# The experts' opening: the second batch's first group normalized by VectorE, its second group's statistics a block later, weight low parts in three pieces

## What is computed

```python
x = x + _L0_attn_ref(_layernorm(x), ...)      # Mamba block and MLP
x = x + _L0_ffn_ref(_layernorm(x), ...)       # table weights
x = x + _L1_attn_ref(_layernorm(x), ...)      # 16 heads, causal
x = x + _L1_ffn_ref(_layernorm(x), ...)       # 8 experts, two for each token
# _L1_ffn_ref, h = the normalized rows:
logits = h @ router_weight.T + router_bias
top_vals, top_idx = jax.lax.top_k(logits, 2)
top_w = jax.nn.softmax(top_vals, axis=-1)
gate_up = h @ gate_up_proj[e] + gate_up_proj_bias[e]
gate = jnp.minimum(gate_up[..., ::2], 7.0)
up = jnp.clip(gate_up[..., 1::2], -7.0, 7.0)
act = (up + 1.0) * gate * jax.nn.sigmoid(gate * 1.702)
out = sum over the token's two experts of  top_w * (act @ down_proj[e] + down_proj_bias[e])
```

## Time and profile before

| | us |
|---|---|
| median of three runs | 1742.09 |
| lowest and highest of them | 1737.66, 1743.52 |
| the profiled execution | 1745.71 |
| its span in the trace | 1744.0 |
| busy in the span: TensorE, VectorE, ScalarE, GpSimd | 1574.2, 1210.8, 981.1, 636.5 |

### The profile page before, as it was taken

One profiled execution on the slowest core, in us unless ns is written; L12 is line 12 of the kernel. 1 busy time (PEld: TensorE's weight loads), 2 busy tenths in 40 slices (PEclk: granted clock), 3 DMA queues, 4 the chain that ended last, 5 costly groups with the idle time before them and its releaser, 6 DMA issues.

```text
span 1744.0 us, 31019 instructions
## 1 busy us (share of the span) xinstructions
PE 1574.2 (90%) x9482; PEld 1327.3 (76%) x9482; DVE 1210.8 (69%) x2671; ACT 981.1 (56%) x2094; POOL 636.5 (36%) x666
## 2 busy tenths in 40 slices
PE   3599998889999899999999999999999998978895
PEld 2366766677888688888888888788888886866784
DVE  6777746789756766667666767766666667668685
ACT  2466654456433476657666765566666665555453
POOL 4333455344334322223322332232233222575632
PEclk9799998999999899999999999999999999999998
DMA  3000012000100600000000000010000000232344
GB/s 103 13 1 1 2 49 67 13 13 7 22 1 1 165 25 25 1 24 24 24 0 24 24 25 1 9 42 1 24 24 24 0 24 7 72 125 75 125 140 133
DMA packets 78388, 64.60 MB, mean 37 GB/s; under 512 B 16656, under 2 KB 72704, under 8 KB 78288
## 3 DMA queue, kind: packets, MB, share of 16 engines
q1 hardware_dynamic: 74544, 53.08, 10.8%
q0 software_dynamic: 3744, 10.26, 1.6%
HBM read 44.89 MB, written 18.43 MB: 36 GB/s over the span
## 4 chain that ended last, share of the span: by engine, by line
PE 60%; DVE 16%; issue 9%; ACT 5%; POOL 4%; DVEq 3%; DMA 1%; POOLq 1%; SPq 0%; ACTq 0%
PE psum L54 9%; PE psum L56 9%; PE psum L55 9%; PE psum L1834 6%; PE psum L1847 4%; PE psum L1850 4%; PE psum L1848 4%; PE psum L1824 3%; PE psum L1825 3%; PE psum L1826 3%; DVE table_leaves L599 2%; DVE mamba_conv_sum L1197 2%; POOL moe_results L2668 2%; DVE attn_probs L1955 1%; DVE gated_hidden L472 1%
## 5 line engine op out<-in xcount | busy, mean ns | idle before, releaser
L2037 POOL TENSOR_SCALAR attn_probs<-attn_probs,attn_inverse 128x128 f32<-128x128 f32 (+7 forms) x256 | 192.3, 752 | 500.2 <-DVE attn_inverse L1985 499.9
L1905 ACT ACTIVATE attn_probs<-attn_probs,attn_neg_max 128x128 f32<-128x128 f32 (+7 forms) x256 | 198.4, 775 | 146.3 <-DVE attn_neg_max L1955 144.8
L1900 ACT ACTIVATE attn_pt_hi<-psum 128x512 fp32r<-128x512 f32 (+3 forms) x384 | 185.3, 483 | 165.4 <-PE psum L1834 164.8
L1951 DVE TENSOR_TENSOR attn_pt_lo<-psum,attn_pt_hi 128x512 fp32r<-128x512 f32 (+3 forms) x384 | 212.0, 553 | 42.4 <-ACT attn_pt_hi L1900 39.6
L1834 PE MATMUL psum<-ident,attn_probs 128*128 128x128 f32 x1152 | 191.7, 276 | 22.8 <-DVE x_tok L1994 12.6
L1955 DVE CUSTOM_DVE_ANT_0 attn_probs<-psum,attn_mask 128x128 f32<-128x128 f32 (+7 forms) x256 | 192.8, 753 | 15.1 <-PE psum L1826 5.9
L1834 PEld LDWEIGHTS psum<-ident,attn_probs 128*128 128x128 f32 x1152 | 141.3, 141 | 48.8 <-DVE attn_pt_lo L1951 13.1
L1847 PE MATMUL psum<-attn_pt_hi,attn_v_hi 128*128 128x512 f32 (+3 forms) x384 | 160.5, 418 | 15.8 <-ACT attn_z_raw L1915 9.0
L427 POOL TENSOR_TENSOR gated_h_lo<-gated_hidden,gated_h_hi 128x512 fp32r<-128x512 f32 x56 | 79.1, 1413 | 156.1 <-ACT gated_h_hi L412 156.1
L1850 PE MATMUL psum<-attn_pt_hi,attn_v_lo 128*128 128x512 f32 (+3 forms) x384 | 134.5, 350 | 0.0
L1824 PE MATMUL psum<-attn_k_hi,attn_q_hi 128*128 128x512 f32 (+3 forms) x384 | 132.5, 345 | 1.8 <-DVE attn_neg_max L1955 1.5
(11 more groups left out here) (384 smaller groups left out, 4707.3 us busy)
## 6 DMA issues: line engine op xcount, KB each, us to landing
moe_xrow<-moe_slots_x SPq DMA_DIRECT2D x46, 129.0 KB, 2.3
moe_slots_x<-attn_z_raw SPq DMA_DIRECT2D x4, 1032.0 KB, 12.2
attn_qkv_raw<-in_L_attn_W_Q_dram SPq DMA_DIRECT2D x32, 128.0 KB, 2.2
attn_qkv_raw<-in_L_attn_W_K_dram SPq DMA_DIRECT2D x32, 128.0 KB, 2.5
attn_qkv_raw<-in_L_attn_W_V_dram SPq DMA_DIRECT2D x32, 128.0 KB, 2.6
attn_wo_raw<-in_L_attn_W_O_dram SPq DMA_DIRECT2D x16, 256.0 KB, 3.1
moe_weights_raw<-_L_ffn_gate_up_proj_dram SPq DMA_DIRECT2D x8, 512.0 KB, 5.3
x_in<-_attn_hidden_states_dram SPq DMA_DIRECT2D x4, 512.0 KB, 5.8
```

Source lines behind the costliest of these rows:

```text
L1900: act.activation(destination(e)[0], work_view(e), ACT.Copy).then_inc(work_hi, 1)
L1905: act.activation(probs_view(e), probs_view(e), ACT.Exp, bias=stat(neg_max, e), scale=-1.0, accum_out=stat(sums, e)).then_inc(exp_done, 1)
L1951: dve.tensor_tensor(lo, work_view(e), hi.bitcast(F32), ALU.subtract).then_inc(work_done, 1)
L2037: pool.tensor_scalar(probs_view(e), probs_view(e), stat(inverse, e), 1.0, ALU.mult, ALU.mult).then_inc(probs_ready, 1)
```

## The change

The norm of the second batch's first group ("apply" 0) goes from GpSimd, where it waited for the attention's end, to VectorE. The second group's statistics ("stats" 1) go from block 0 to block 1, and its norm ("apply" 1), still on GpSimd, from block 1 to block 2. `low` makes its subtraction in pieces of 512 words: one instruction, as before, for the pieces of experts 0 to 3, three instead of one for experts 4 to 7; the semaphore is raised by the last.

```diff
@@ ExpertWeights.low
-        pool.tensor_tensor(lo, raw, hi.bitcast(F32), ALU.subtract).then_inc(self.split_lo, 1)
+        step = self.half // self.PIECES
+        for at in range(0, n, step):
+            last = pool.tensor_tensor(lo[:, at:at + step], raw[:, at:at + step], hi[:, at:at + step].bitcast(F32), ALU.subtract)
+        last.then_inc(self.split_lo, 1)
@@ moe_stage
-    LATE = {0: [("apply", 0), ("stats", 1)], 1: [("apply", 1), ("turn", 0)], 2: [("turn", 1)], 3: [("turn", 2)],
+    LATE = {0: [("apply", 0)], 1: [("stats", 1), ("turn", 0)], 2: [("apply", 1), ("turn", 1)], 3: [("turn", 2)],
@@ moe_stage, gpsimd, late
-            elif step == "apply":
-                if m == 0:
-                    pool.wait_ge(*attention["done"])
+            elif step == "apply" and m:
                 norm["apply_rows_gpsimd"](pool, GROUPS + HALF + m)
@@ moe_stage, vector, late
             if step == "stats":
                 norm["stats"](dve, group)
+            elif step == "apply" and m == 0:
+                dve.drain()
+                norm["apply"](dve, group)
```

## The result

| | before | after |
|---|---|---|
| median (11 runs each, made together) | 1743.52 | 1748.32 |
| lowest, highest | 1737.66, 1746.70 | 1746.30, 1750.74 |
| span of the profiled execution | 1744.0 | 1748.1 |

The changed kernel is slower: the ratio is 1.0037, its 95% interval 1.0025 to 1.0048, so about 6.4 us on the earlier time (4.4 to 8.4); the medians themselves are 4.8 apart. The forecast was +6.1, or 1748.2 us from the earlier median of 1742.09.

What follows compares the result with a forecast made beforehand. The experts' opening was taken as bound by a chain of waits through GpSimd, TensorE, ScalarE and VectorE, not by TensorE. The late second norm, +5.7, and the pieces, +0.4, gave +6.1: 1748.2 us, range 1743.0 to 1752.0.

Steps and rivals of the forecast that it cites:

- Part 1: Experts' opening: first group's norm on VectorE lets TensorE's turning start at 1563.2 in place of 1565.97, 2.8 us earlier.
- Part 2: Second group's statistics a block later on VectorE: block 2's `moe_gate` at 1568.6 before 1570.51, 1.9 us left of 2.8.
- Part 3: Second group's norm on GpSimd behind expert 4's low parts: ends at 1580.5, block 4's `moe_gate` at 1585.1, +5.7 us.
- The clock: TensorE at half clock after its over 8 us wait: 4.6 us to block 4's `moe_gate`; at full clock, half of 4.5 goes.
- rival (a): Clock stays full in the long wait, or VectorE regains most of blocks 5 and 6: 3 to 4 us, about 1746; 20%.
- Rival (b): Second group's norm in block 2 costs nothing, rows ready when TensorE asks; kernel faster by 3 or so, 1739; 7%.
- Part 4: Three pieces for low parts of experts 4 to 7: between -2.7 and +1.7, taken as +0.4 us for longer subtractions.
- Rival (c): Pieces worsen the lock, holding `moe_th` then `moe_hidden`, up to 1.7 more; low clock into block 5, another 1 to 2: 1751; 16%.
- The sum of the parts: +5.7 for the late second norm and +0.4 for the pieces: +6.1 us at block 7, 1748.2 us on the median.
- Rival (d): Behind block 7, the shift is taken up in the stage of scatters and stores: 0 to +2, 1743; 5%.
- The chances: Whole kernel: slower by over 0.3% 55%, within 0.3% 38%, faster 7%; the forecast itself 52%.
- only the subtractions held it: Block 2's `moe_th` ran in 0.43 beside GpSimd's norm, so the norm doesn't hold VectorE, against the skill's shared-port rule.

Runs made afterwards that it cites:

- Experiment 1: Changed kernel with the second group's norm right behind its root on GpSimd, ahead of expert 4's low parts: 1744.33 us, ratio 1.0008 to the kernel before.
- experiment 6: Changed kernel with the second group's norm another step later, behind expert 5's low parts too: 1755.48 us, ratio 1.0063 to the kernel before.
- experiment 5: Changed kernel with 34 unread 512-column products on TensorE ahead of its wait for the second group's rows: 1746.0 us, ratio 1.0017 to the kernel before.
- experiment 7: Kernel before with the first group's norm on VectorE and the three pieces, without later statistics and later norm: 1742.58 us, ratio 0.9996.
- experiment 8: Kernel before with the first group's norm on VectorE and blocks 5 and 6's `moe_th` in PSUM, low parts in one piece: 1737.07 us, ratio 0.9967.
- experiment 2: Kernel before with only the three pieces for the low parts of experts 4 to 7: 1740.18 us, ratio 0.9996.

## Why the prediction was right

**Part 1, first turning.** Right. It was to start 3.3 us behind block 0's `moe_gate` (1563.2 against 1559.86); it did at 3.44, with 1.05 of idle where under 1 was forecast. The four L206 took 1.38 for the 1.37 of the earlier trace rows.

**Part 2, block 2.** Right. Forecast 1568.6, which is 8.7; measured 8.86. Since the clock stayed up, VectorE alone set it, as assumed.

**Part 3, the term that decides.** The mechanism is the one forecast, row by row: GpSimd's order is root, root, three pieces, four L224, and TensorE waits for the last, "over 8 us", 9.19 in fact. Experiment 1 took some 5 us off the time (3.9 at block 4 in its trace) by moving these four instructions alone, and experiment 6 added 5.1 by putting one more expert ahead of them. The norm ended at 21.4 behind block 0's `moe_gate`, forecast 20.6. The step mis-sized is the seam: I set 0.1 between the last piece and the first L224, and it was 0.87 ("issue" in the row). The start that I had for such a seam, 1567.23 in the earlier trace rows with 0.20 ahead of it, came right behind other L224 with only a root between; it wasn't a like case. A `pool.drain()` stands ahead of the four L224 in both kernels (L220). By the trace it ended 0.73 behind the last piece, and in the kernel before 0.08 behind the root, so it is most of the seam. Block 4 came at +6.47, forecast +5.7, so nearly all of the 0.8 is this.

**The clock.** Low behind the wait, as taken: from the turning to block 4's `moe_gate` it was 4.43 us for the forecast's 4.6. What the low clock costs was over-sized: I had put half of the 4.5, 2.2 us, on it, and experiment 5, at full clock, needed 2.88 from the turning (1579.08) to `moe_gate` (1581.96), so 1.5. Not all of that stretch is TensorE's work. Neither half of rival (a) occurred: the clock fell, and VectorE got little of blocks 5 and 6 back, as the next part shows. Rival (b), no cost, fell with the wait of 9.19.

**Part 4, the pieces.** Between -2.7 and +1.7 I took +0.4; from block 4 to block 7 the difference went from +6.47 to +6.19, so -0.3 (block 7 is at 40.68; the forecast's 1600.5 is 40.64). Both things that the part weighed happened: `moe_th` came down from 1.53 and 2.05 to 1.15 and 0.95, and at block 6 `moe_hidden` was held for 1.33. Rival (c) named this second hold; it was right that it occurs and wrong on the price, since the first holds grew smaller by more (0.4 and 1.1) than the second hold cost (0.9). The sum of the parts, +6.1 for +6.19 measured, owes its closeness to luck: two errors of some 0.7 with opposite signs.

**Behind block 7.** Rival (d), that the shift is absorbed by the scatters, fell: +6.18 at the scatter's start. At the end of the loop it is +5.4 (184.14 and 189.52), but that says nothing of the change: the stretch from block 7 to the end took 146.2 to 149.7 us over the ten traces, though its instructions are the same in all ten.

**The chances.** The 55% for a kernel slower by over 0.3% doesn't follow from the parts that the prediction names: two thirds of 52 and nearly all of 16 are about 50, and 43 are left for the middle in place of 38.

**The rule on the shared ports.** The Trainium skill (SBUF — State Buffer, section "SBUF: two separate sides") would have GpSimd's L224 hold VectorE's operations with two SBUF inputs as the subtractions do. In the changed kernel VectorE does nothing beside them, but other traces agree with the prediction that they don't, nearly: beside L224 of 1.2 each, `moe_hidden` took 0.61 at block 0 of the kernel before and 0.62 in experiment 1, and `moe_th` 0.53 in experiments 7 and 8, in place of 0.43. So the prediction's "only the subtractions held it" leaves out 0.1 to 0.2. The subtractions did hold it, as the rule says. The section limits the lock to VectorE instructions with two SBUF inputs or in a mode that takes both ports, and experiment 8 agrees: with one input in PSUM, VectorE ran at 0.43 inside a subtraction of 3.50. Which of its modes L206 was in when it was held (experiment 8) no run here shows.

## What to carry to other kernels

Where engines take work in order, a step that is moved to "a block later" also moves past all that the other engine's queue has in that block: list for each engine what now stands ahead of it, and how long that runs, before asking what the move saves. A moved producer costs what stands ahead of it only from the point where its consumer becomes late; here 2.74 us in which GpSimd was free, ahead of expert 4's weights, were left unused. Where a VectorE operation with two SBUF inputs was held by a long GpSimd subtraction, putting one input in PSUM removed the hold, and cutting the subtraction in pieces mostly moved it.

## What the runs showed that was not expected

- The first L224 on GpSimd starts 0.87 us after the instruction ahead of it has ended (0.95 in experiment 6), whether that is a subtraction (1575.17 above) or a root (1564.59 in experiment 1, where the root ended at 1563.72); it was 0.20 only where other L224 had run just ahead of the root. Of the 0.87, 0.73 pass until the drain ahead of the L224 has ended. Why the drain took 0.08 in the one case and 0.73 in the other isn't shown, and no run leaves it out. Putting this norm between two subtractions thus cost nearly a microsecond beyond its duration.
- An operation of VectorE with two SBUF inputs is held for whole pieces, sometimes for more than one (2.50), and its successor may be held by the next piece (1.33). In experiment 2 and the changed kernel `moe_th` at block 3 got in (0.46, 0.44), in experiment 7 at block 3 it got in (0.46) and at block 4 it did not. In the two cases of the changed kernel in which it got in, it ended 0.28 behind the end of a piece, and the piece that followed took 1.44 in place of 1.27 to 1.29.
- With the tanh in PSUM both operations took 0.43 and 0.42 beside subtractions of 3.50 and 3.47. With one SBUF input and an SBUF output, L206 was held all the same (1.37 for 0.41).
- After the long wait the granted clock stayed at 0.50 for some four microseconds of work; around a wait of 1.05 us it fell in two executions and not in three others with the same instructions up to there.
